# Projection stage of a hybrid attention layer: betas and sums of squares as rows, A ahead of the q convolution, the substitution in buffers of its own

## The chip, the cores and the metric

The kernel runs on one core of one Trainium2 chip. The metric is the device time of one execution in microseconds (us): 16 sequences of 1024 tokens with 256 channels, all in f32 at the interface. A smaller time is better. Engines are called PE (TensorE), DVE (VectorE), ACT (ScalarE), POOL (GpSimd) and SP (SyncE, which only issues DMAs here).

## The reference, cut to what matters

Each sequence passes a delta-rule attention with a router, a slot network, a softmax attention and the slot network again. The change touches the first part of the first one:

```python
q = silu(dw_causal_conv(x @ Wq, conv_q_w))      # 4 taps, k and v alike
beta = sigmoid(x @ Wb)                          # 4 heads of 64 channels
q, k = l2norm(q), l2norm(k); v = v * beta; kb = k * beta
T = -einsum('bhnid,bhnjd->bhnij', kb, k)        # chunks of 32 tokens, strictly lower part
for i in range(1, 32):
    T[..., i, :i] += einsum('bhnj,bhnji->bhni', T[..., i, :], T[..., :, :i])
T = T + eye(32)                                 # inverse of a unit triangular matrix
local_out = dw_causal_conv(v_raw, local_w)      # 7 taps
mid_out = dw_causal_conv(v_raw, mid_w)          # 25 taps
```

## The kernel before

A loop body of some 530 us runs 16 times, once for each sequence. It calls seven stages, each a block in which every engine has its own program, with semaphores between them and a meeting of all engines at the end. `project_and_convolve` (L399 to L729) is the first, followed by `delta_rule`. All intermediate tensors stay in SBUF; `bounce` is a buffer in HBM through which blocks change their layout.

PE multiplies the normed input, channels in the partitions, with Wk, Wv and Wq (L539, units of 512 tokens in four PSUM banks; unit u waits for the evacuation of unit u - 4). Between the q units stand the betas (L515), with the input as the stationary operand and four columns moving. ACT evacuates to `pre` (L603) and makes the first tap (L620), DVE the other three (L678), two halves of 128 channels each. The accumulators of k and q share `k_tm`. ACT takes silu (L609) and squares of k and q (L613). PE sums the squares over a head in small products (L509) and forms the gram matrices of k (`gram`, L528, pairs of banks). DVE turns them into `negd`, minus beta over the sum of squares, and multiplies the grams with it into A (L700). For the reciprocal roots POOL raises both sums to the power -1/2 in one instruction (L444). PE transposes k and v to tokens in the partitions (L501), ACT copies them out (L626).

SP's queue is written out by hand, and each wait in it holds all that stands behind it: 32 copies of v into `rep` (L456), four shifts of eight channel groups, 16 for each channel half; A's four diagonal blocks to `bounce` (L465); the gather of all 32 x 32 blocks into `block_a`, one in each partition (L472), which needs `delta_tm`, where v stood; after the substitution the solution X and its transpose XT to `bounce` (L475, L477) and seven scatters back, into `Xd` and `TT` (L483, L485).

The substitution (L391, L393) goes over 31 columns, two dependent DVE instructions each, in `block_a`, X and the scratch `product`. Beside it PE makes the 25-tap convolution as four units of products of 32 columns on `rep` and `stack` (L576), transposes its result (L588), then the 7-tap convolution in four short units and its transposes. ACT keeps each unit (L655) and each transposed piece (L665); the last go to `local_tm`, where X and XT lie, so they wait for `inverse_out`. DVE ends with the transposed copy of X (L711), four sums over heads for the router (L715, L717) and the scaled v (L721, L722). `keep_warm` (L312) issues products whose result nobody reads.

## Time and profile before

| | us |
|---|---|
| median of 3 runs | 8511.21 (8493.76 to 8513.71) |
| profiled execution, as timed | 8544.68 |
| its span, first to last instruction | 8543.0 |
| PE busy | 7615.2 (89%) |
| DVE busy | 4873.9 (57%) |
| ACT busy | 3364.6 (39%) |
| POOL busy | 1774.2 (21%) |
| mean granted clock of PE | 0.937 of 2.4 GHz |

The shares are means over seven stages with different limits. An f32 product stands in the trace as two instructions, and busy PE includes the warming products. All times in rows are us from the start of the span. An arrow names what ended an engine's idle time. A DMA is shown where SP issues it.

### The profile page before, as it was taken

The numbers are of one execution on the slowest core, as the hardware profiler recorded it, in microseconds if no ns is written. First come the engines' busy times: TensorE is split into PE (matmuls) and PEld (weight loads), VectorE is DVE, ScalarE is ACT, GpSimd is POOL, SyncE is SP. The second block draws the span as 40 slices with busy tenths as digits, with TensorE's granted clock in tenths as the row PEclk, the third lists the DMA queues.
The fourth block names the chain that finished last, engine by engine and source line by source line (L and its number), as shares of the span: only waits on it lengthen the run. The fifth ranks groups of instructions, "written<-read, shape, count | busy, mean of one in ns | idle before, by whom it ended". The sixth has DMA issues, their size and how long they took to land. (4 is left out here: it accounts for less than half of the span.)

```text
span 8543.0 us, 124391 instructions
## 1 busy us (share of the span) xinstructions
PE 7615.2 (89%) x48654; PEld 4524.8 (53%) x48654; DVE 4873.9 (57%) x9442; ACT 3364.6 (39%) x6843; POOL 1774.2 (21%) x2657
## 2 busy tenths in 40 slices
PE   6899988999889889998988998988889988998889
PEld 4546455464654646546464464644646546465464
DVE  5465665556655566554665546655466554655546
ACT  2252532525335253342533425334253342534425
POOL 2112121121211222112221122211222112221212
PEclk9999999999999999999999999999999999999999
DMA  2011111201112021110211102111021110211102
GB/s 71 16 34 27 31 45 22 42 13 31 45 23 43 10 36 40 30 40 8 36 40 31 45 1 36 40 31 45 1 36 40 31 45 1 36 40 31 45 1 41
DMA packets 337643, 268.66 MB, mean 31 GB/s; under 512 B 213378, under 2 KB 276226, under 8 KB 336954
## 3 DMA queue, kind: packets, MB, share of 16 engines
q1 hardware_dynamic: 337004, 260.04, 15.3%
q8 instruction: 414, 6.78, 0.4%
q14 instruction: 225, 1.84, 0.1%
HBM read 48.66 MB, written 42.02 MB: 11 GB/s over the span
## 5 line engine op out<-in xcount | busy, mean ns | idle before, releaser
L1731 ACT ACTIVATE sa_pt<-ps 128x512 f32<-128x512 f32 (+3 forms) x3072 | 1272.0, 492 | 740.3 <-PE ps L1719 734.8
L1656 DVE TENSOR_REDUCE sa_nm<-ps 128x2 f32<-128x1024 f32 (+4 forms) x1280 | 1390.3, 1114 | 285.8 <-PE ps L1637 138.2
L1719 PE MATMUL ps<-sa_qs,sa_ks 99*128 99x512 bf16 (+3 forms) x3072 | 803.4, 336 | 76.1 <-ACT sa_pt L1731 58.3
L1637 PE MATMUL ps<-sa_ks,sa_qs 96*128 96x512 bf16 (+3 forms) x2560 | 642.5, 325 | 47.6 <-DVE sa_nm L1656 33.3
L1738 POOL TENSOR_SCALAR_AFFINE_SELECT sa_pt<-sa_pt 128x512 f32<-128x512 f32 x512 | 325.1, 635 | 1707.7 <-ACT sa_pt L1731 1705.2
L312 PE MATMUL ps<-identb 128*128 128x512 bf16 x2656 | 645.4, 391 | 10.5 <-ACT dr_z L1001 10.5
L1751 PE MATMUL ps<-sa_pt,sa_va 128*17 128x512 f32 (+3 forms) x6144 | 645.8, 492 | 8.2 <-POOL sa_pt L1738 8.2
L1719 PEld LDWEIGHTS ps<-sa_qs,sa_ks 99*128 99x128 bf16 x3072 | 259.3, 98 | 655.4 <-ACT sa_pt L1731 473.7
L576 PE MATMUL ps<-rep,stack 128*32 128x512 f32 x4608 | 501.0, 593 | 0.0
L280 POOL TENSOR_TENSOR rstd<-vare,mhalf 128x2 f32<-128x2 f32 x260 | 181.0, 696 | 1251.2 <-DVE vare L272 1251.2
L797 POOL TENSOR_TENSOR A<-paths 128x256 f32<-128x256 f32 x384 | 272.1, 742 | 802.5 <-DVE paths L967 802.5
L287 ACT ACTIVATE xn<-x,shift,rstd 128x256 f32<-128x256 f32 x520 | 278.2, 592 | 403.7 <-POOL shift L282 403.4
L312 PEld LDWEIGHTS ps<-identb 128*128 128x128 bf16 x2656 | 262.3, 103 | 304.1 <-issue 48.0
L678 DVE SCALAR_TENSOR_TENSOR k_tm<-pre,cw,k_tm 128x1024 f32<-128x1024 f32 x192 | 245.2, 1284 | 226.8 <-ACT k_tm L620 222.2
L1637 PEld LDWEIGHTS ps<-sa_ks,sa_qs 96*128 96x128 bf16 x2560 | 244.4, 99 | 230.2 <-DVE sa_nm L1656 70.1
L1081 DVE COPY ro_partial<-ps 128x512 f32<-128x512 f32 x32 | 22.1, 691 | 558.3 <-PE ps L1113 558.3
L1641 PE MATMUL ps<-causal,identb 128*128 128x128 bf16 x1792 | 339.0, 222 | 0.0
L1219 PE MATMUL ps<-ident,paths 128*128 128x128 f32 x2048 | 269.7, 299 | 67.1 <-DVE paths L1183 67.1
L576 PEld LDWEIGHTS ps<-rep,stack 128*32 128x32 f32 x4608 | 146.5, 110 | 334.9 <-issue 334.9
L319 PE MATMUL ps<-ident,xn 128*128 128x128 f32 x784 | 139.2, 353 | 197.5 <-PEq L1297 77.6
L1175 POOL TENSOR_TENSOR mi_scale<-mi_ms,mhalf 128x16 f32<-128x16 f32 x32 | 92.8, 2899 | 1008.1 <-DVE mi_ms L1188 1008.1
L1219 PEld LDWEIGHTS ps<-ident,paths 128*128 128x128 f32 x2048 | 264.1, 214 | 68.7 <-DVE paths L1183 68.7
(344 smaller groups left out, 14553.2 us busy)
## 6 DMA issues: line engine op xcount, KB each, us to landing
sa_qs<-sa_parts SPq DMA_DIRECT2D x288, 128.0 KB, 4.4
sa_ks<-sa_parts SPq DMA_DIRECT2D x288, 128.0 KB, 5.7
x<-in_x SPq DMA_DIRECT2D x17, 1024.0 KB, 5.6
rep<-paths SPq DMA_DIRECT2D x128, 128.0 KB, 2.3
bounce<-paths SPq DMA_DIRECT2D x32, 512.0 KB, 2.7
out_y<-x SPq DMA_DIRECT2D x32, 512.0 KB, 3.0
rep<-paths SPq DMA_DIRECT2D x128, 127.9 KB, 2.4
rep<-paths SPq DMA_DIRECT2D x128, 127.8 KB, 2.3
```

The source lines that it names most:

```text
L287: return nc.scalar.activation(k.xn[:, t, 0:D], x[:, t, :], ACT.Identity, bias=k.shift[:, t:t + 1], scale=k.rstd[:, t:t + 1])
L312: nc.tensor.matmul(scratch, k.identb[:, 0:P], k.identb[:], start=True, stop=True)
L576: last = nc.tensor.matmul(ps[CG * g:CG * (g + 1), 4 + u % 4, :], k.stack[:, (base + j) * GROUPS + gg, :], rep[:, gg, PAD + n * BANK - SHIF ...
L797: nc.gpsimd.tensor_tensor(with_delta[:, t % 2, 1 + n, :], m.delta_tm[:, t, :], paths[n][:, t, :], ALU.mult).then_inc(s.d_products, 1)
L1219: last = nc.tensor.matmul(ps[:, HALVES * n + a, j * P:(j + 1) * P], paths[i][:, n * TN + j, a * P:(a + 1) * P], k.ident[:], start=(i == 0 ...
L1637: last = nc.tensor.matmul(cols[:, i, :], qs[0:NCOMB * AD, g % NBUF, op.j + i, op.t * P:(op.t + 1) * P], ks[0:NCOMB * AD, g % NBUF, op.j + ...
L1641: last = nc.tensor.matmul(cols[:, i, op.w - P:], k.identb[:, 0:P], k.causal[:], start=False, stop=True, skip_group_check=True)
L1656: nc.vector.tensor_reduce(nm[:, g % 2, op.c, op.t, op.j:op.j + op.heads], cols, AX.X, ALU.max, negate=True).then_inc(s.slot_free, 1)
L1719: last = nc.tensor.matmul(bank[:, off:], ks[0:QROWS, g % NBUF, j, kt * P:(kt + 1) * P], qs[0:QROWS, g % NBUF, j, n * BANK + off:(n + 1) * ...
L1731: nc.scalar.activation(pt[:, gs % 2, j, off:BANK], ring_bank(ring_use(gs, j))[:, off:], ACT.Exp, scale=RATIO).then_inc(s.ring_out, 1)
L1738: nc.gpsimd.affine_select(block, block, [[0, GH], [1, P]], ALU.is_ge, 0.0, base=0, channel_multiplier=-1).then_inc(s.masked, 1)
L1751: last = nc.tensor.matmul(ps[2 * AD * j:2 * AD * j + AD + 1, SUM_BANK, off:BANK], va[:, kt, g * GH + j, :], pt[:, gs % 2, j, off:BANK], st ...
```

## The change

Heads now stand in the partitions and tokens along the row: `wb`, padded to 32 columns, is stationary, the input moves 512 tokens at a time, and the four products (two halves of tokens by two halves of channels) go to four strips of 32 partitions of one bank. The sums of squares do the same with `ones2` of 32 columns, added for k onto the betas' rows. ACT copies these rows to SBUF (`keep_rows`), and a product with the selector `pick` turns them into tokens in the partitions (`pick(i)`).

k's sums are taken, A is made, and only then DVE convolves q, whose accumulator is now `mid_tm`. On ACT silu of k moves among the v pieces. On SP A's blocks leave after the first 16 copies; the gather goes into the scratch part of `TT` (the memory of `pre`, so it waits for q's convolution) and stands ahead of the last eight copies. The first pair of DVE's sums moves ahead of the substitution, q's sums are read after its 16th column, POOL's power becomes one instruction for k and one for q. At the end `Xd` is scattered before `TT`, 7-tap units are ordered by token halves, and their transposes and copies come in two halves. In the core of the diff new lines prevail; lines that went are in the code above.

```diff
...
+    return (*two_squares(TT.rearrange("p t n -> p (t n)")[:, 0:2 * CHUNK * CHUNK]),
+            *two_squares(m.local_tm.rearrange("p t d -> p (t d)")))
...
+    accs = [channel_major(m.k_tm[:]), channel_major(m.v_tm), channel_major(m.mid_tm)]
+    BEHIND = 2 * (3 + L) + 2
+    sq = [channel_major(m.local_tm),
+          pre[:].rearrange("p i a l -> p (i a l)")[:, BEHIND:BEHIND + HALVES * L].rearrange("p (a l) -> p a l", a=HALVES)]
...
+    ROWS, PICKED = (7, 0), (6, 1)
...
+    units = [(0, a, n) for a in range(HALVES) for n in range(NB)] + [(1, a, n) for n in range(NB) for a in range(HALVES)]
...
+            pool.wait_ge(s.rows_ps, 1)
...
+            pool.wait_ge(s.ss, 1)
+            nc.gpsimd.tensor_tensor(m.rn[:, 0, :], m.ss[:, 0, :], k.mhalf[:, 0:T * H], ALU.pow).then_inc(lc.rnorm, 1)
+            pool.wait_ge(s.turned, T)
+            pool.wait_ge(s.rep0, 16 * SHIFTS * (P // CG))
+            pool.wait_ge(s.rep1, 16 * SHIFTS * (P // CG))
+            nc.gpsimd.memset(Xd[:], 0.0).then_inc(lc.zeroed, 1)
+            pool.wait_ge(s.rows_ps, 2)
+            nc.gpsimd.memset(TT[:, scratch:], 0.0).then_inc(lc.zeroed, 1)
             pool.wait_ge(s.ss, 2)
-            nc.gpsimd.tensor_tensor(m.rn[:], m.ss[:], k.mhalf[:].rearrange("p (i n) -> p i n", i=2),
-                                    ALU.pow).then_inc(lc.rnorm, 1)
+            nc.gpsimd.tensor_tensor(m.rn[:, 1, :], m.ss[:, 1, :], k.mhalf[:, 0:T * H], ALU.pow).then_inc(lc.rnorm, 1)
             pool.wait_ge(lc.inverse, 1)
-            nc.gpsimd.memset(Xd[:], 0.0).then_inc(lc.zeroed, 1)
+            nc.gpsimd.memset(TT[:, 0:scratch], 0.0).then_inc(lc.zeroed, 1)
...
+            copies(0, range(SHIFTS))
             sp.wait_ge(s.a, T)
...
-            sp.wait_ge(s.rep0, 16 * SHIFTS * (P // CG))
+            copies(1, range(SHIFTS // 2))
             sp.wait_ge(s.blocks_out, 16 * BLOCKS)
-            block_a = substitution_tensors(m)[0]
-            sp.wait_ge(s.turned, T)
+            sp.wait_ge(s.conv, 3 * HALVES)
             sp.dma_start(block_a, bounce[0].rearrange("b g r c -> (b g) r c")).then_inc(lc.blocks, 16)
+            copies(1, range(SHIFTS // 2, SHIFTS))
...
-            sp.dma_start(bounce[2].rearrange("b g r c -> (b g) r c"), XT).then_inc(lc.inverse_out, 16)
-            sp.wait_ge(lc.inverse_out, 32)
-            sp.wait_ge(lc.zeroed, 2)
+            sp.dma_start(bounce[2].rearrange("b g r c -> (b g) r c"), XT).then_inc(lc.turned_out, 16)
+            sp.wait_ge(lc.inverse_out, 16)
+            sp.wait_ge(lc.zeroed, 1)
+            for b in range(BLOCKS - 1):
+                left = CHUNK * (b % 2)
+                sp.dma_start(by_blocks(Xd, 2 * CHUNK)[rows(b), :, left:left + CHUNK],
+                             bounce[1, b].rearrange("g r c -> r g c")).then_inc(lc.inverse_in, 16)
+            sp.wait_ge(lc.turned_out, 16)
+            sp.wait_ge(lc.zeroed, 3)
...
+            def betas():
+                for n in range(NB):
+                    for a in range(HALVES):
+                        nc.tensor.matmul(ps[rows(2 * n + a), ROWS[0], :], k.wb[:, a, :],
+                                         k.xnT[:, a, n * BANK:(n + 1) * BANK], start=True, stop=False, skip_group_check=True)
+            def sums_of_squares(i):
+                pe.wait_ge(s.squared, HALVES * (i + 1))
+                for n in range(NB):
+                    for a in range(HALVES):
+                        last = nc.tensor.matmul(ps[rows(2 * n + a), ROWS[i], :], k.ones2[:],
+                                                sq[i][:, a, n * BANK:(n + 1) * BANK], start=(i == 1), stop=True,
+                                                skip_group_check=True)
+                last.then_inc(s.rows_ps, 1)
...
+            def pick(i):
+                pe.wait_ge(s.rows, i + 1)
+                for j in range(NT):
+                    last = nc.tensor.matmul(ps[:, PICKED[i], j * PICKS[i]:(j + 1) * PICKS[i]], rows_of[i][:, j * P:(j + 1) * P],
+                                            k.pick[:, 0:PICKS[i]], start=(j == 0), stop=True, skip_group_check=True)
+                last.then_inc(s.picked, 1)
...
-                if i == 0:
-                    pe.wait_ge(s.a, 6)
                 for u in range(T // 2):
-                    if i == 1:
+                    if i == 0:
+                        pe.wait_ge(s.a, (4, 4, 6, 6)[u])
+                        pe.wait_ge(s.pre, 3 * HALVES * NB)
+                    else:
                         pe.wait_ge(s.tm, u + 1)
...
+            betas()
+            for a in range(HALVES):
+                project(2, k.wq, a)
+            sums_of_squares(0)
             pe.wait_ge(s.silu, HALVES)
             gram(0)
+            pick(0)
+            pe.wait_ge(s.pre, 10)
+            gram(1)
             pe.wait_ge(s.pre, 3 * HALVES * NB)
-            gram(1)
-            sums_of_squares(0, 0)
             gram(2)
-            sums_of_squares(0, 1)
-            pe.wait_ge(s.tanh, 1)
-            keep_warm(nc, k, ps[:, AB, :], 6)
+            keep_warm(nc, k, ps[:, ROWS[0], :], 3)
             pe.wait_ge(s.a, 2)
             gram(3)
-            pe.wait_ge(s.ss, 1)
-            for a in range(HALVES):
-                sums_of_squares(1, a)
-            to_token_major(0)
-            to_token_major(1)
-            keep_warm(nc, k, ps[:, AB, :], 4)
+            for i in range(2):
+                to_token_major(i)
+            keep_warm(nc, k, ps[:, ROWS[0], :], 4)
             pe.wait_ge(s.padded, 2)
             pe.wait_ge(s.a, T)
-            pe.wait_ge(s.ss, 2)
...
+                if u == 1:
+                    pe.wait_ge(s.tm, T)
+                    sums_of_squares(1)
+                if u == 2:
+                    pick(1)
+                if u == 4:
+                    pe.wait_ge(lc.evac, 4)
+                    pe.wait_ge(s.ss, 2)
+                    turn_path(0, range(T // 2))
+                if u == 6:
+                    pe.wait_ge(lc.evac, 6)
+                    turn_path(1, range(T // 4))
+            pe.wait_ge(lc.evac, 8)
+            turn_path(1, range(T // 4, T // 2))
             keep_warm(nc, k, ps[:, 4, :], 8)
...
+            def keep_rows(i):
+                act.wait_ge(s.rows_ps, i + 1)
+                nc.scalar.activation(rows_of[i], ps[:, ROWS[i], :], ACT.Copy).then_inc(s.rows, 1)
...
+            for a in range(HALVES):
+                evacuate(0, a)
+                first_tap(0, a)
+            for a in range(HALVES):
+                evacuate(1, a)
+                first_tap(1, a)
+                silu(0, a)
+            silu(1, 0)
+            for a in range(HALVES):
+                square(0, a)
+            silu(1, 1)
+            act.wait_ge(io.stored, 16 * NB)
+            keep_rows(0)
+            evacuate(2, 0)
+            act.wait_ge(s.ss, 1)
+            nc.scalar.activation(by_halves(m.beta[:]), picked(0, 1), ACT.Tanh, scale=0.5).then_inc(s.tanh, 1)
+            first_tap(2, 0)
+            evacuate(2, 1)
+            first_tap(2, 1)
+            to_token_major(0, m.k_tm[:])
+            to_token_major(1, m.v_tm)
+            silu(2, 0)
+            act.wait_ge(s.tm, T)
+            nc.scalar.activation(m.ev[:], m.v_tm, ACT.Square).then_inc(lc.square, 1)
+            silu(2, 1)
+            for a in range(HALVES):
+                square(1, a)
+            keep_unit(0)
+            keep_unit(1)
+            keep_rows(1)
+            keep_unit(2)
+            keep_unit(3)
+            keep_path(0, m.mid_tm, range(T // 2))
+            keep_unit(4)
+            act.wait_ge(lc.summed, 1)
+            act.wait_ge(lc.tm, T // 2)
+            nc.scalar.activation(m.ev[:], m.mid_tm, ACT.Square).then_inc(lc.square, 1)
+            keep_unit(5)
+            keep_unit(6)
+            act.wait_ge(lc.inverse_out, 16)
+            act.wait_ge(lc.turned_out, 16)
+            keep_path(1, m.local_tm, range(T // 4))
+            keep_unit(7)
+            keep_path(1, m.local_tm, range(T // 4, T // 2))
...
-            for i in range(3):
+            for i in range(2):
                 convolve(i)
+            dve.wait_ge(s.picked, 1)
+            nc.vector.tensor_scalar(by_halves(m.ss[:, 0, :]), picked(0, 0), 1e-12, None, ALU.add).then_inc(s.ss, 1)
...
+            settle(nc.vector.reciprocal(m.negd[:], m.ss[:, 0, :]))
...
+            settle(nc.vector.scalar_tensor_tensor(m.negd[:], m.negd[:], -1.0, m.beta[:], ALU.mult, ALU.mult))
...
-            nc.vector.tensor_copy(XT, X.rearrange("p i j -> p j i")).then_inc(lc.inverse, 1)
+            convolve(2)
...
+            def feature_sums(i, path):
                 dve.wait_ge(lc.square, i + 1)
                 nc.vector.tensor_reduce(early[:, :, 3 - i, :], m.ev[:].rearrange("p t (h d) -> p t h d", h=H), AX.X, ALU.add)\
                     .then_inc(lc.summed, 1)
                 nc.vector.tensor_reduce(early[:, :, 1 - i, :], path.rearrange("p t (h d) -> p t h d", h=H), AX.X, ALU.add)
+            feature_sums(0, m.v_tm)
+            dve.wait_ge(s.unit, 2)
+            dve.wait_ge(lc.blocks, 16)
+            settle(substitute(nc, dve, settle, tensors, range(CHUNK // 2)))
+            dve.wait_ge(s.picked, 2)
+            nc.vector.tensor_scalar(by_halves(m.ss[:, 1, :]), picked(1, 0), 1e-12, None, ALU.add).then_inc(s.ss, 1)
+            substitute(nc, dve, settle, tensors, range(CHUNK // 2, CHUNK - 1)).then_inc(lc.inverse, 1)
+            dve.wait_ge(lc.inverse, 1)
+            nc.vector.tensor_copy(XT, X.rearrange("p i j -> p j i")).then_inc(lc.inverse, 1)
...
```

## Rows read from the trace of the kernel before

**Rows 1.** window of the stage: us; busy PE, PEld, DVE, ACT, POOL; clock; DMA; GB/s
```profile
600.00:698.30 98.30, 87.93 (x581) 47.66 (x579) 64.07 (x101) 41.64 (x56) 17.26 (x7) 0.90 0.35 81
```

**Rows 2.** who DVE's substitution waited for, whole span: us, times
```profile
  DMA paths<-bounce: 196.0, 16
```

**Rows 3.** timeline of DVE: start us, us, line, operands, count [idle before <-releaser]
```profile
620.99 7.76 DVE L678 SCALAR_TENSOR_TENSOR paths<-pre,cw,paths 128x1024 f32<-128x1024 f32 x6
...
633.52 3.93 DVE L678 SCALAR_TENSOR_TENSOR k_tm<-pre,cw,k_tm 128x1024 f32<-128x1024 f32 x3 [0.55 <-ACT k_tm L620]
...
639.89 0.19 DVE L692 TENSOR_SCALAR ss<-ps 128x32 f32<-128x32 f32 x1 [2.35 <-PE ps L509]
...
640.94 4.87 DVE L700 TENSOR_TENSOR A<-ps,negd 128x512 f32<-128x512 f32 x8
...
660.95 0.22 DVE L391 TENSOR_TENSOR paths<-paths 128x31 f32<-128x31 f32 x1 [12.55 <-DMA paths<-bounce]
...
673.17 0.43 DVE L391 TENSOR_TENSOR paths<-paths 128x255 f32<-128x255 f32 x1
...
684.39 2.67 DVE L711 COPY paths<-paths 128x1024 f32<-128x1024 f32 x1
...
695.97 2.29 DVE L722 TENSOR_TENSOR x<-paths,e 128x2048 f32<-128x2048 f32 x1
```

**Rows 4.** timeline of SyncE's queue, the same stage
```profile
630.05 21.43 SPq L456 DMA_DIRECT2D rep<-paths  x32
651.53 2.82 SPq L465 DMA_DIRECT2D bounce<-A  x4
656.95 0.34 SPq L472 DMA_DIRECT2D paths<-bounce  x1
...
690.12 0.32 SPq L483 DMA_DIRECT2D paths<-bounce  x1
```

**Rows 5.** timeline of PE, the same stage
```profile
614.60 7.03 PE L539 MATMUL ps<-xnT,wv 128*128 128x512 f32 x16
...
633.88 1.95 PE L509 MATMUL ps<-ones,paths 128*128 128x2 f32 x16
635.75 1.16 PE L528 MATMUL ps<-kT 64*128 64x128 f32 x16
...
648.03 3.50 PE L501 MATMUL ps<-ident,kT 128*128 128x128 f32 x16
...
654.07 24.24 PE L576 MATMUL ps<-rep,stack 128*32 128x512 f32 x224
...
692.71 3.36 PE L588 MATMUL ps<-ident,xn 128*128 128x128 f32 x16 [4.71 <-ACT xn L655]
695.91 1.89 PE L312 MATMUL ps<-identb 128*128 128x512 bf16 x8
```

**Rows 6.** timeline of ScalarE, the same stage
```profile
623.52 1.28 ACT L609 ACT_TABLE_LOAD   x1
...
626.73 1.06 ACT L603 ACTIVATE pre<-ps 128x512 f32<-128x512 f32 x2
627.87 1.15 ACT L620 ACTIVATE k_tm<-pre,cw 128x1024 f32<-128x1024 f32 x1
```

**Rows 7.** busy time of PE in two stretches: us, busy, clock, DMA share, GB/s
```profile
637.00:643.50 6.50, 6.50 (x32) 0.54 0.77 174
651.00:688.00 37.00, 36.28 (x328) 1.00 0.23 54
```

**Rows 8.** timeline in the fourth pass, POOL and DVE
```profile
1702.24 10.54 POOL L444 TENSOR_TENSOR rn<-ss,mhalf 128x64 f32<-128x64 f32 x1 [7.17 <-DVE ss L705]
...
1711.61 0.22 DVE L393 TENSOR_TENSOR paths<-paths 128x31 f32<-128x31 f32 x1
```

**Rows 9.** timeline in the delta rule of the second pass, POOL and DVE
```profile
730.53 2.16 POOL L790 TENSOR_TENSOR dr_squares<-paths 128x256 f32<-128x256 f32 x3
...
731.46 1.52 DVE L936 TENSOR_TENSOR dr_r<-dr_r,x 128x256 f32<-128x256 f32 x1
```

More of the change, by code:

```diff
@@ L145, in _ @@
                     (k.rw2[0:HLAST, HC - 1, :], w["rw2"][(HC - 1) * P:HID]),
-                    (k.rb2, w["rb2"]), (k.gather, w["gather"]),
+                    (k.rb2, w["rb2"]), (k.gather, w["gather"]), (k.pick, w["pick"]),
                     (k.ident, w["ident"]), (b_raw[:, 0:4 * P], w["identb"]),
@@ L420, in out_cm @@
         return k.xn[:, r:r + n // D, 0:D] if n >= D else k.xn[:, r, c:c + n]
-    units = [(c, a, n) for c in range(2) for a in range(HALVES) for n in range(NB)]
+    units = [(0, a, n) for a in range(HALVES) for n in range(NB)] + [(1, a, n) for n in range(NB) for a in range(HALVES)]
     def rows(b):
@@ L459, in _ @@
             sp.wait_ge(s.padded, 2)
-            copies(0)
-            copies(1)
+            copies(0, range(SHIFTS))
             sp.wait_ge(s.a, T)
@@ L490, in _, with project @@
         def _(pe):
+            def project(i, w, a):
+                for n in range(NB):
+                    u = (i * HALVES + a) * NB + n
+                    if u >= 4:
+                        pe.wait_ge(s.pre, u - 3)
+                    for c in range(HALVES):
+                        last = nc.tensor.matmul(ps[:, u % 4, :], w[:, c, a * P:(a + 1) * P],
+                                                k.xnT[:, c, n * BANK:(n + 1) * BANK],
+                                                start=(c == 0), stop=(c == HALVES - 1))
+                    last.then_inc(s.proj, 1)
+            def betas():
[5 more added lines that the diff above has]
+                pe.wait_ge(s.squared, HALVES * (i + 1))
+                for n in range(NB):
+                    for a in range(HALVES):
[9 more added lines that the diff above has]
+                last.then_inc(s.picked, 1)
             def to_token_major(i):
                 pe.wait_ge(s.silu, HALVES * (i + 1))
-                if i == 0:
-                    pe.wait_ge(s.a, 6)
                 for u in range(T // 2):
-                    if i == 1:
+                    if i == 0:
+                        pe.wait_ge(s.a, (4, 4, 6, 6)[u])
+                        pe.wait_ge(s.pre, 3 * HALVES * NB)
+                    else:
                         pe.wait_ge(s.tm, u + 1)
@@ L503, in to_token_major @@
                     last.then_inc(s.turned, 1)
-            def sums_of_squares(i, a):
-                pe.wait_ge(s.squared, HALVES * i + a + 1)
-                for t in range(T):
-                    first = SS[i].start + t * H + 2 * a
-                    last = nc.tensor.matmul(ps[:, SUMS, first:first + 2], sq[i][:, a, t * P:(t + 1) * P], k.ones2[:],
-                                            start=(i == 0 and a == 0 and t == 0), stop=True, skip_group_check=True)
-                last.then_inc(s.sums, 1)
-            def betas(t):
-                for c in range(HALVES):
-                    last = nc.tensor.matmul(ps[:, AB, t * H:(t + 1) * H], k.xnT[:, c, t * P:(t + 1) * P],
-                                            k.wb[:, c, :], start=(t == 0 and c == 0), stop=(c == HALVES - 1),
-                                            skip_group_check=True)
-                if t == T - 1:
-                    last.then_inc(s.beta, 1)
             def gram(u):
@@ L703, in _ @@
                         bc(m.negd[:, 2 * u * H + odd:(2 * u + 2) * H:2], P), ALU.mult).then_inc(s.a, 1)
-            dve.wait_ge(s.sums, 2 * HALVES)
-            nc.vector.tensor_scalar(m.ss[:, 1, :], ps[:, SUMS, SS[1]], 1e-12, None, ALU.add).then_inc(s.ss, 1)
-            dve.wait_ge(s.unit, 2)
-            dve.wait_ge(lc.blocks, 16)
-            substitute(nc, dve, settle, m, range(CHUNK - 1)).then_inc(lc.inverse, 1)
-            dve.wait_ge(lc.inverse, 1)
-            nc.vector.tensor_copy(XT, X.rearrange("p i j -> p j i")).then_inc(lc.inverse, 1)
+            convolve(2)
             early = early_features(m)
-            for i, path in enumerate((m.v_tm, m.mid_tm)):
+            def feature_sums(i, path):
                 dve.wait_ge(lc.square, i + 1)
@@ L2003 @@
     "io": "loaded stored",
-    "pc": "padded proj pre tap conv silu beta tanh turned tm squared sums ss gram a blocks_out unit rep0 rep1",
-    "lc": "blocks square summed conv evac turned tm zeroed rnorm inverse inverse_out inverse_in",
+    "pc": "padded proj pre tap conv silu squared rows_ps rows picked tanh ss gram a turned tm blocks_out unit rep0 rep1",
+    "lc": "blocks square summed conv evac turned tm zeroed rnorm inverse inverse_out turned_out inverse_in",
     "dr": "zeroed products square summed d_products d_square d_summed at_ps at5 at6 y5_ps z "
@@ L2118, in laid_out @@
     i, j = np.arange(P)[:, None], np.arange(P)[None, :]
+    half, wanted, col = (np.arange(4 * H)[None, :] // H) % NB, np.arange(4 * H)[None, :] // (NB * H), np.arange(4 * H)[None, :] % H
+    group, row = i // CG, i % CG
+    of_sum = (wanted == 0) & (row == col % HALVES) & (group == HALVES * half + col // HALVES)
+    of_beta = (wanted == 1) & (row == H + col) & (group // HALVES == half)
     order = (2, 6, 0, 3, 7, 1, 8, 10, 12, 4, 5, 9, 11, 13)
```

171 lines of the change are left out of this document (59 added, 112 removed).

## Prediction

> **What bounds the kernel now.** I read the busy times of one projection stage first [rows 1]. The body runs 16 times and this is its second pass: 98.3 us, in which PE shows 87.9 us and VectorE (DVE) 64.1. PE looks like the bound, but part of its time is warming products and small products that spread over waits for others, so the share doesn't decide. The waits do [rows 2]: DVE sat idle for 196.0 us over 16 passes before the substitution, for a DMA. The reader should see in DVE's timeline [rows 3] one nearly closed chain: v convolution to 628.75, q convolution to 637.45, A from 640.94 to 645.81, then nothing that matters until 660.95, substitution to 684.36, the transposed copy, four sums (8.9 us with the small product behind them), and the scaled v, which ends last at 698.26. In SyncE's queue [rows 4] the hole has a cause: 32 copies of v into rep take 630.05 to 651.48 (0.67 each); A's four block copies stand behind them and leave at 651.53 though A was ready at 645.81; the gather leaves at 656.95, and lands 4.0 later. PE [rows 5] has finished all 224 products of the wide convolution at 678.3, six us ahead of the substitution, and then waits for ScalarE, whose squares wait for DVE. So the stage is set by DVE and SP in turn; PE has little slack. The stage is of one shape in every pass, so a saving counts 16 times.
>
> **The change, from the front.** Times are on the clock of this pass.
> PE's k and v projections end at 614.60 + 7.03 = 621.6 as now [rows 5]. Betas: 8 products on four column strips (the trace shows an f32 product as two). The wide convolution does 224 such in 24.24, 0.108 each, so 0.9. The q projection is now without the small beta products: 16 products at 0.43 = 6.9, to 629.4; as now it ended at 631.9, 2.5 are gained. Sums of squares as rows: 0.9, to 630.3. By then ScalarE has made what they need. The table load (1.3, [rows 6]) and one silu (estimate 1.1, a pass over 1024 as the tap's 1.15) move ahead of the last v pieces, so the last v tap ends at 624.7, which DVE reaches at 624.87: covered by 0.2, no more, and a later one would push the whole chain. Squares are done at about 628.5, silu of v at 629.8.
> The rows then go through ScalarE (0.6) and, behind gram(0), PE (4 picks, 8 products; the sums of squares of now have the nearest form, 16 in 1.95 [rows 5], so 1.0), to 632.3. From the read of the sums to A lie 1.05 now (639.89 to 640.94, [rows 3]), and one operation falls out while beta's comes in: A starts at 633.3. ScalarE meanwhile evacuates q (two pairs of 1.1 about a tap of 1.15 [rows 6], and tanh); its last piece is out at 635.0, and gram(2) waits for it. gram(2), three warming products and gram(3), which also waits for A's bank, follow. At PE's full clock (16 products in 1.1) A ends at 639.2. The rows show the clock at 0.54 in 637 to 643.5 [rows 7], after a stretch of thin products; at the half level gram(2), the warmers and gram(3) take 5.4 instead of 2.8, and A ends at 641.9. I take the middle, **640.5, 5.3 earlier than 645.81**.
> A rule of the Trainium skill bears here (TensorE: Matmul & The Clock Gate, Why this matters for your kernels): don't leave TensorE idle in mid-kernel, or it drops to its lower clock. It speaks against three warmers in place of six. By it A would end at the 641.9 above and everything behind would be 1.4 later, 8.6 a pass and 8373 in all; by the full clock it would be 8330.
>
> q convolution: 2 x 3.93 = 7.8, to 648.3. SP: 16 copies start when silu of v's first half is done, 626.7, and end at 637.4, before A. Block copies 640.5 to 643.3 (2.8, [rows 4]); eight copies to 648.7; gather at 648.7, landed 4.0 later: **652.7**. The last eight copies are issued by 654.4 and landed by 656.7 (2.3 more, as from the last block copy's end at 654.35 to the gather's issue at 656.95). DVE fills the hole: q convolution, then the first two sums, 4.5, to 652.8. So a hole of 12.6 becomes 0, and substitution starts at **652.8 instead of 660.95: 8.1 earlier**. It can't start before 650.7 even with A at 638, nor with the gather as now after 655 if A slips to 643.
> Sixteen columns take 12.2 (660.95 to 673.17), to 665.0, and then DVE wants the second pick. PE: transposes of k after gram(3), 3.5 as now at the half clock, of v half as long, 1.8, warmers 1.0 (eight take 1.9), wide convolution from about 645.5 instead of 654.07, two units of 6.06, row sums 0.9, third unit to 664.6, pick to 665.6. DVE loses 0.7 and 0.2 for the sum; the other 11.2 bring it to **t = 677.2, against 684.36: 7.2 earlier**. PE is now second by under 1 us: here the cover is gone.
>
> **The tail.** Now it takes 13.9 from t. After: DVE has copy 2.67, one pair of sums 4.5, 0.2 and 2.3: t + 9.7. SP: the second solution leaves at t + 2.7 and is out 3.0 later (from the transposed copy's end at 687.06 to the next issue at 690.12, [rows 4]); only then four copies of 0.7 and 2.6 to land: t + 11.1. ScalarE and PE: two copies, the last unit, then at the half clock (3.36 for 16) eight transposes 1.7 and eight warmers 1.9: t + 11.1. The three copies into Xd leave in the gap and cost nothing. POOL's memsets hide behind DVE. I take t + 11.1 with bounds 9.7 (DVE alone) and 12.9 (the warmers at half clock too): **the tail gives 2.8**, bounds 1.0 and 4.2.
>
> Sum: 7.2 + 2.8 = **10.0 us a pass, x 16 = 160 us**. Setup gains one small load and wider weights: nothing against 16 passes. The profiled execution took 8543.0 us of span, 8544.7 as timed; it becomes about 8385. That execution stands 33 above the median of the runs, 8511.2, so the prediction is 8511 - 160 = **8351 us**.
>
> **Rivals.**
> 1. *POOL's power takes DVE's port.* It becomes two instructions of 32 columns, half of 10.54 [rows 8], 5.3 each, one beside the first small products of DVE and one in the middle of the substitution. An addition of DVE with two operands in SBUF, 256 elements wide, took 1.52 when it met a run of POOL's products, and ended 0.3 after the last of them [rows 9]; an operation of that width in the substitution takes 0.43 [rows 3]. If the power acts so, A starts about 5 later but mostly behind the grams, so 2.5 net, and the substitution loses 5.3: 10.0 - 7.8 = 2.2 a pass, 8476. Against it stands [rows 8]: once in this trace the gather came early and the substitution ran for 1.4 us inside the power, its operations 0.22 as ever. That is the last part of a long instruction; its start has not been seen. Chance 0.12. The Trainium skill (SBUF — State Buffer, Who interferes with whom) has this as a rule: a DVE instruction with two SBUF inputs contends with a GpSimd instruction that reads SBUF. Rows 9 agree, rows 8 don't.
> 2. *PE or the queue becomes the bound.* Copies, block copies and the gather share the DMA engines (0.77 busy in [rows 7]); PE starts the wide convolution cold, or rep's second half lands late. Three to six us later at the middle of the substitution: 4 to 7 a pass, 8399 to 8447. For it: PE's slack of 0.7. Chance 0.17.
> 3. *The other side: the clock stays at its half level in the wide convolution.* The three units before the pick, now 18, would take 36: +18 - 10.0 = 8.0 later a pass, 8639. It decides once PE loses more than 10 us there, two units out of three. Against it: the clock was 1.00 in 651 to 688 [rows 7], and these products are dense. Chance 0.03.
> 4. *It does nothing.* The rows' round trip through ScalarE and PE could eat what the order gives: A would have to start 10 later, at 643, which no term above comes near, or several costs meet. Chance 0.04.
> 5. *All goes well*: A at 639.2, PE warm, tail 9.7: 8.5 + 4.2 = 12.7 a pass, 8308; with PE's slack used up little more. Chance 0.10.
> My own case, 8310 to 8395 as its own range: 0.54.
>
> The range takes in 5, the own case and 2, and leaves out 1, 3 and part of 4: **8300 to 8450**. A measurement of this kernel tells 0.3% (26 us) from no change (three runs spread over 20). Faster by more: 0.93 (all but 3 and 4); within 0.3%: 0.04; slower: 0.03.
>
> **What would show it.** DVE's wait for the gather under 2 us instead of 12.6; A's last product near 640; one product of A waiting for gram(2); the power beside substitution operations of unchanged 0.42; PE's wait inside the wide convolution for rep under 1; the stage about 88 long from first projection to the last of DVE instead of 98. Wrong it would be made by a substitution that has a hole of 5 in its middle (rival 1, or the pick late), by granted clock 0.5 after 645, or by a gather that takes well over 4 us beside the copies.

## The result, and the profile after

| | before | changed |
|---|---|---|
| median of 4 runs each, us | 8503.83 (8493.76 to 8513.71) | 8379.37 (8347.73 to 8388.70) |
| profiled execution, as timed | 8544.68 | 8374.86 |
| its span | 8543.0 | 8373.1 |
| mean granted clock of PE | 0.937 | 0.950 |

The ratio is 0.9837, with a 95% interval of 0.9818 to 0.9856: 1.6% faster. The medians differ by 124.5 us, the two profiled spans by 169.9; the profiled execution of before stands 41 above its median, that of the changed kernel 5 below.

The second pass now begins its projections at 590.46, where that of before began at 605.04. DVE's timeline, to be laid beside [rows 3]:

```profile
606.43 7.76 DVE L733 SCALAR_TENSOR_TENSOR paths<-pre,cw,paths 128x1024 f32<-128x1024 f32 x6
618.24 0.19 DVE L745 TENSOR_SCALAR ss<-ps 128x32 f32<-128x32 f32 x1 [4.05 <-PE ps L538]
...
619.07 0.19 DVE L750 SCALAR_TENSOR_TENSOR negd<-negd,beta 128x32 f32<-128x32 f32 x1
619.29 2.48 DVE L754 TENSOR_TENSOR A<-ps,negd 128x512 f32<-128x512 f32 x4
621.93 1.29 DVE L754 TENSOR_TENSOR A<-ps,negd 128x512 f32<-128x512 f32 x2 [0.16 <-PE ps L564]
623.78 1.29 DVE L754 TENSOR_TENSOR A<-ps,negd 128x512 f32<-128x512 f32 x2 [0.56 <-PE ps L564]
624.98 7.76 DVE L733 SCALAR_TENSOR_TENSOR paths<-pre,cw,paths 128x1024 f32<-128x1024 f32 x6
632.66 2.28 DVE L764 TENSOR_REDUCE prob<-x 128x32 f32<-128x2048 f32 x1
634.85 2.27 DVE L766 TENSOR_REDUCE prob<-paths 128x32 f32<-128x2048 f32 x1
639.40 0.21 DVE L388 TENSOR_TENSOR pre<-paths,pre 128x31 f32<-128x31 f32 x1 [2.27 <-DMA pre<-bounce]
...
652.63 0.19 DVE L773 TENSOR_SCALAR ss<-ps 128x32 f32<-128x32 f32 x1 [1.05 <-PE ps L538]
652.74 0.42 DVE L388 TENSOR_TENSOR pre<-paths,pre 128x255 f32<-128x255 f32 x1
...
663.95 2.65 DVE L776 COPY paths<-paths 128x1024 f32<-128x1024 f32 x1
...
671.10 2.29 DVE L782 TENSOR_TENSOR x<-paths,e 128x2048 f32<-128x2048 f32 x1
```

The q convolution and two sums now lie between A and the substitution, in the place of the hole of 12.55. Two small waits are left: 2.27 for the gather, and a new one of 1.05 in the middle, for the second pick (the product with the selector that turns q's sums). Over the span the first is 32.2 us, against the 196.0 of [rows 2]:

```profile
  DMA pre<-bounce: 32.2, 16
```

SP's queue, beside [rows 4]. A's blocks no longer stand behind 32 copies, and the gather no longer behind all of them:

```profile
612.07 10.15 SPq L473 DMA_DIRECT2D rep<-paths  x16
625.09 2.60 SPq L481 DMA_DIRECT2D bounce<-A  x4
627.74 6.32 SPq L473 DMA_DIRECT2D rep<-paths  x8
634.17 0.51 SPq L487 DMA_DIRECT2D pre<-bounce  x1
634.73 4.96 SPq L473 DMA_DIRECT2D rep<-paths  x8
663.94 0.35 SPq L491 DMA_DIRECT2D bounce<-paths  x1
...
669.65 2.64 SPq L503 DMA_DIRECT2D pre<-bounce  x4
```

PE, beside [rows 5]. Betas and both sums of squares take 1.1 each, a pick as much. PE waits 2.53 inside the wide convolution for the last copies of `rep`, and the unit behind that wait takes 7.75, where each unit took 6.06 before. The pick that DVE waits for stands behind both:

```profile
606.99 1.06 PE L523 MATMUL ps<-xnT,wb 128*32 128x512 f32 x8
...
615.05 1.07 PE L530 MATMUL ps<-paths,ones 128*32 128x512 f32 x8
...
617.13 1.07 PE L538 MATMUL ps<-pick,x 128*128 128x16 f32 x8
...
643.78 7.75 PE L609 MATMUL ps<-rep,stack 128*32 128x512 f32 x56 [2.53 <-DMA rep<-paths]
651.46 1.06 PE L538 MATMUL ps<-pick,paths 128*128 128x8 f32 x8
...
672.26 1.89 PE L312 MATMUL ps<-identb 128*128 128x512 bf16 x8
675.12 0.63 PE L893 MATMUL ps<-ident,A 128*128 128x128 f32 x4 [0.97 <-PEq L439]
```

The busy time by windows (us, busy and count of PE, PEld, DVE, ACT, POOL, clock, DMA share, GB/s), to be set against the 0.54 of [rows 7] at the grams:

```profile
612.00:622.00 10.00, 8.57 (x73) 5.25 (x72) 5.62 (x11) 7.86 (x11) 4.59 (x3) 1.00 0.80 181
628.00:634.00 6.00, 6.00 (x58) 1.85 (x60) 5.93 (x5) 4.47 (x5) 0.00 (x0) 1.00 0.87 176
640.00:646.00 6.00, 3.47 (x24) 0.72 (x20) 5.42 (x18) 1.19 (x2) 2.12 (x2) 0.79 0.35 69
643.80:646.80 3.00, 3.00 (x16) 0.77 (x20) 2.76 (x8) 0.00 (x0) 2.92 (x2) 0.50 0.00 0
647.00:652.00 5.00, 5.00 (x49) 1.63 (x41) 4.23 (x11) 0.39 (x1) 0.42 (x1) 1.00 0.00 0
```

The last two rows say why the third unit is long: after its wait PE works without a gap, but for 3 us at half the clock.

And POOL, for the first rival. Both powers run beside DVE's operations of L750 and L388 above, which last 0.19 and 0.42 as ever:

```profile
618.51 5.43 POOL L453 TENSOR_TENSOR rn<-ss,mhalf 128x32 f32<-128x32 f32 x1 [1.14 <-DVE ss L745]
...
652.90 5.53 POOL L462 TENSOR_TENSOR rn<-ss,mhalf 128x32 f32<-128x32 f32 x1 [5.48 <-DVE ss L773]
```

One pass is not the mean, so the next table gives the means over the 16 passes, worked out from the timelines and counted from each pass's first projection product. "Flight" is from the gather's issue to the substitution's first operation; "t" is the substitution's end; "stage" ends where PE begins to load the delta rule's first product.

| kernel | A made | gather issued | flight | subst. starts | 17th column | t | DVE ends | stage |
|---|---|---|---|---|---|---|---|---|
| before | 39.92 | 51.61 | 4.11 | 55.72 | 67.93 | 79.12 | 93.01 | 93.36 |
| changed | 34.34 | 43.47 | 4.94 | 48.41 | 61.76 | 72.95 | 82.43 | 84.35 |
| changed again | 34.60 | 43.81 | 4.98 | 48.79 | 62.20 | 73.39 | 82.88 | 84.75 |
| e1, old tail | 34.43 | 43.65 | 4.89 | 48.54 | 62.04 | 73.23 | 82.74 | 85.75 |
| e2, q before A | 41.91 | 50.88 | 4.98 | 55.86 | 68.35 | 79.55 | 89.04 | 91.62 |
| e3, gather last | 34.30 | 49.23 | 4.23 | 53.46 | 65.79 | 76.98 | 86.43 | 89.62 |
| e4, sum read at 20 | 34.57 | 43.76 | 4.96 | 48.72 | 60.94 | 72.24 | 81.98 | 83.45 |
| e5, last warmers out | 34.18 | 43.40 | 5.04 | 48.44 | 61.75 | 72.94 | 82.42 | 84.00 |
| e6, POOL products | 34.50 | 43.68 | 4.89 | 48.57 | 61.96 | 75.72 | 85.18 | 88.03 |
| e8, gather alone | 34.41 | 43.61 | 3.63 | 47.24 | 64.39 | 75.58 | 85.06 | 87.76 |
| e9, six copies, 20 | 34.49 | 42.49 | 4.75 | 47.24 | 59.46 | 70.78 | 81.60 | 82.15 |
| e10, front warmers out | 33.62 | 42.84 | 4.90 | 47.74 | 61.56 | 72.76 | 82.24 | 84.67 |
| e11, e9 and e10 | 33.73 | 41.72 | 4.78 | 46.50 | 58.71 | 70.00 | 80.85 | 81.22 |
| e12, small products | 39.05 | 47.40 | 7.31 | 54.71 | 67.04 | 78.23 | 87.71 | 90.66 |

The stage went from 93.36 to 84.35: 9.0 a pass, 144 us of the 169.9 by which the spans differ. The rest lies in the other stages, whose code is the same. The medians differ by less than 144; what that leaves open stands below, with the step table.

### The profile page after: what moved, and what is told of

It is laid out like the page before. It is cut to its first block and busy times, and to the rows that moved or that the text cites. A ratio compares the mean times of both kernels' runs of the same rounds, so it can differ in the third digit from the quotient of the medians.

```text
span 8373.1 us, 122632 instructions
## 1 busy us (share of the span) xinstructions
PE 7421.8 (89%) x47710; PEld 4285.2 (51%) x47710; DVE 4866.4 (58%) x9426; ACT 3367.4 (40%) x6875; POOL 1783.2 (21%) x2689
## 5 line engine op out<-in xcount | busy, mean ns | idle before, releaser
L312 PE MATMUL ps<-identb 128*128 128x512 bf16 x2608 | 626.9, 388 | 10.4 <-ACT dr_z L1061 10.4
L609 PE MATMUL ps<-rep,stack 128*32 128x512 f32 x4608 | 529.2, 611 | 41.9 <-DMA rep<-paths 41.9
L312 PEld LDWEIGHTS ps<-identb 128*128 128x128 bf16 x2608 | 253.3, 101 | 297.8 <-issue 42.3
L850 POOL TENSOR_TENSOR dr_squares<-paths 128x256 f32<-128x256 f32 x384 | 283.5, 774 | 0.0
```

Source lines behind the costliest of these rows:

```text
L312: nc.tensor.matmul(scratch, k.identb[:, 0:P], k.identb[:], start=True, stop=True)
L609: last = nc.tensor.matmul(ps[CG * g:CG * (g + 1), 4 + u % 4, :], k.stack[:, (base + j) * GROUPS + gg, :], rep[:, gg, PAD + n * BANK - SHIF ...
L850: nc.gpsimd.tensor_tensor(squares[:, t0 % 2, 1 + n, :], paths[i][:, t0, :], paths[j][:, t0, :], ALU.mult).then_inc(s.products, 1)
```

## The experiments

Each is an edit of the changed kernel. Medians and ratios are against the kernel before on the same chip, whose medians lay between 8510 and 8534 there. The changed kernel itself was run again:

> The changed kernel itself once more, as the standard for the three beside it: 8380 within 10 us, 0.984 of the kernel before.

Measured: 8402.81 us, 0.9872 (0.9857 to 0.9887), stage 84.75, so outside what I expected. The stages agree within 0.4 us, while the ratio lies 0.35 points above the first one. Outside the 16 stages the two spans agree within 1 us, but that of e2 is 29 lower there, that of e5 34 higher and that of before 26 higher, though none of these edits touches the code there. So differences under some 30 us between kernels are read below from the stage, not from the median.

**e1, the old tail.** Scatters interleaved as before, 7-tap units, transposes and copies not in halves.

```diff
-    units = [(0, a, n) for a in range(HALVES) for n in range(NB)] + [(1, a, n) for n in range(NB) for a in range(HALVES)]
+    units = [(c, a, n) for c in range(2) for a in range(HALVES) for n in range(NB)]
...
+                if b < 3:
+                    left = CHUNK * (b % 2)
...
```

> The changed kernel with the end of the stage as before: the scatters into Xd and TT interleaved behind both stores, the 7-tap units in the old order, their transposes and copies all behind the last unit. The stage from the first projection to the first product of the delta rule is 84.35 us as a mean over the passes in the changed kernel and 93.36 before. My theory (the tail by halves gives 2.8 of the 9.0 a pass, since the scatters of Xd leave the path): the stretch from the substitution's end to the next stage goes from 11.4 back to 14.2 and the kernel gets 45 us slower than the changed one, about 8425. Rival (the warmers and the last transposes would hide it): under 10 us slower.

Measured: 8394.91 (8388.16 to 8403.30), 0.9865 (0.9849 to 0.9882). From t to the stage's end 12.52, against 11.40 changed and 14.24 before. So order and halves give 1.1 us a pass. In e1 the last scatter lands 0.46 before the next stage in all 16 passes, and PE ends 4.1 or more ahead of it (8.0 after t, 10.9 in the changed kernel). By the trace, then, the 1.1 come from the scatters' order, and the halves, with the last unit kept behind the wait for the solution, made PE end later. Neither was run alone. The other 1.7 of the tail's 2.8 are there without them: DVE needs 9.5 from t instead of 13.9, since a pair of sums went into the gather's wait. My expectation, that all of the tail's gain hangs on the halves, was too high.

**e2, the q convolution ahead of A.** One line moved.

```diff
+            convolve(2)
             for u in range(T // 2):
...
-            convolve(2)
```

> The changed kernel with DVE's convolution of q ahead of the products into A again; rows, buffers and tail as changed. My theory (the order, not the rows, fills the hole): A ends 7.8 us later, its blocks leave behind it, the gather leaves near 50 us from the stage's start and DVE waits some 8 us for it again; the stage is 7 us longer, the kernel 110 us slower than the changed one, near 8490. Rival (the rows' wide products, done by 16 us earlier, and the gather's new place are what paid): less than 50 us slower.

Measured: 8484.71 (8450.44 to 8511.49), 0.9972 (0.9955 to 0.9988). A comes 7.6 later, the substitution 7.5, the stage 7.3. So without the order on DVE four fifths of the 9.0 are lost.

**e3, the gather behind all copies.**

```diff
-            copies(1, range(SHIFTS // 2))
+            copies(1, range(SHIFTS))
...
-            copies(1, range(SHIFTS // 2, SHIFTS))
```

> The changed kernel with all 16 copies of v's second half ahead of the gather, none behind it. If DVE's chain sets the time, the gather leaves 5 us later (48.5 from the stage's start in place of 43.5), the substitution starts 4 to 5 later, and the wait in its middle of 1.1 us disappears, since rep's second half is there early: 3 to 4 us a pass, 50 to 65 us slower than the changed kernel. If the wide convolution of PE is as much the bound (rival), the earlier copies pay back most of it: under 20 us.

Measured: 8451.28 (8444.65 to 8472.16), 0.9935 (0.9914 to 0.9956). The gather leaves 5.8 later and flies 0.7 shorter, so the substitution starts 5.1 later; 1.0 comes back since the second pick is now early enough (12.3 for 16 columns). The stage is 5.3 longer, more than the 3 to 4 expected, with 1.2 of it behind t.

**e10, no warming products around the last gram.** Seven products of L312 taken out.

```diff
-            keep_warm(nc, k, ps[:, ROWS[0], :], 3)
...
-            keep_warm(nc, k, ps[:, ROWS[0], :], 4)
```

> The changed kernel without the three warming products ahead of the last gram and the four ahead of the wide convolution. In the changed kernel the grams ran at the full clock. If the warmers hold it there, then without them the clock falls to its half level somewhere between the grams and the wide convolution: grams and transposes take up to 5 us more, the second pick comes later and the kernel is 30 to 80 us slower than the changed one. If the wide products of the betas and sums did it (rival), the time is the same within 10 us, and PE is 1.8 us earlier at the wide convolution, which only lengthens its wait for rep.

Measured: 8361.93 (8353.50 to 8369.88), 0.9824 (0.9808 to 0.9841). A is made 0.7 earlier, the clock is 1.00 in each window from 600 to 640, and the stage is as long as before the edit. Why, PE's timeline of this kernel says:

```profile
626.66 12.22 PE L607 MATMUL ps<-rep,stack 128*32 128x512 f32 x112
638.71 1.04 PE L530 MATMUL ps<-pre,ones 128*32 128x512 f32 x8
643.57 7.91 PE L607 MATMUL ps<-rep,stack 128*32 128x512 f32 x56 [3.82 <-DMA rep<-paths]
```

Counted from the pass's start PE is 1.9 earlier at the third unit and waits 1.3 longer for `rep`. The unit behind the wait then takes 7.9, in this pass and as the mean (7.4 in the changed kernel), so of PE's 1.9 the pick keeps 0.1. What makes the pick late is the landing of the last copies and, behind it, a stretch at half the clock.

**e4, the sum read after column 20 instead of 16.**

```diff
-            settle(substitute(nc, dve, settle, tensors, range(CHUNK // 2)))
+            settle(substitute(nc, dve, settle, tensors, range(20)))
```

> The changed kernel, but DVE reads q's sums after column 20 of the substitution instead of after 16. In the changed kernel it waits 1.15 us there for the second pick, which waits for PE's third wide unit, which waits for rep's second half. If that wait is all that PE costs, it disappears: 1.1 us a pass, 17 us in all. Rival (what stands behind the sums on PE, the transposes of the 25-tap path, gets late and gives it back in the tail): no change.

Measured: 8368.44 (8347.73 to 8417.45), 0.9833 (0.9806 to 0.9860). The first 16 columns take 12.2 again instead of 13.4, and the stage is 1.3 shorter than that of the changed kernel beside it: the whole mid wait is gone.

**e9, six copies ahead of the gather and ten behind it, with e4's edit.**

```diff
-            copies(1, range(SHIFTS // 2))
+            copies(1, range(6))
...
-            copies(1, range(SHIFTS // 2, SHIFTS))
+            copies(1, range(6, 16))
```

> As the one before, and only six of the second 16 copies stand ahead of the gather, ten behind it. SP was the last to be ready for the gather (it left at 43.5 from the stage's start, q's convolution ends at 42.2). Expected: gather 1.3 us earlier, the substitution too, 2.3 us a pass with the other, 35 to 40 us below the changed kernel. Rival: the gather is held by the copies' traffic and lands at the same time, then 17 as above.

Measured: 8355.74 (8325.07 to 8363.60), 0.9810 (0.9797 to 0.9824). Against the changed kernel beside it the gather leaves 1.3 earlier, t comes 2.6 earlier, and so does the end. But DVE now waits in the tail:

```profile
665.56 2.29 DVE L764 TENSOR_REDUCE prob<-x 128x32 f32<-128x2048 f32 x1 [1.73 <-ACT x L714]
```

**e8, the gather alone.** The last eight copies wait until it has landed.

```diff
+            sp.wait_ge(lc.blocks, 16)
             copies(1, range(SHIFTS // 2, SHIFTS))
```

> The changed kernel, but the last eight copies of v leave only when the gather has landed. The gather took 4.94 us from issue to the substitution's start as a mean in the changed kernel and 4.11 before, where nothing came behind it. If the copies behind it slow it, it takes 4.1 again and the substitution starts 0.8 earlier, but rep's second half lands 5 us later and the wait in the substitution's middle grows from 1.15 to 5 or more: 50 to 70 us slower than the changed kernel. If the copies ahead of it do (rival), the flight stays at 4.9 and the time is later by the same wait and 10 us more.

Measured: 8457.42 (8422.26 to 8476.29), 0.9913 (0.9885 to 0.9941). The flight is 3.6 in every pass, against 4.6 to 5.9 with the eight copies behind it. Nothing else on the queue ahead of the gather was changed, so the copies behind it are what costs 1.3. The price is paid in the middle of the substitution, where the pick is 5 late (PE waits 4.1 for `rep`, and its third unit takes 8.5):

```profile
642.79 0.22 DVE L388 TENSOR_TENSOR pre<-paths,pre 128x31 f32<-128x31 f32 x1 [0.83 <-DMA pre<-bounce]
...
660.05 0.19 DVE L774 TENSOR_SCALAR ss<-ps 128x32 f32<-128x32 f32 x1 [5.08 <-PE ps L539]
```

**e5, the last eight warming products out.**

```diff
-            keep_warm(nc, k, ps[:, 4, :], 8)
```

> The changed kernel without the eight warming products at the end of the stage. PE ended at 674.15 in the profile and the next stage began at 675.12, when the scatters into TT had landed. If SP's scatters end the stage, the stage's length stays; the delta rule's first products then run at the half clock: 0 to 1 us a pass slower. If PE's end counts (rival), 1 to 2 us a pass faster.

Measured: 8408.96 (8390.82 to 8416.51), 0.9869 (0.9854 to 0.9884). The stage is 84.00 against 84.35 and 84.75, and what comes behind, up to the router's first instruction, takes 89.8 against 88.6 and 89.0. The delta rule's first 3.5 us, from 681.80 in the second pass, run at clock 0.50, in the changed kernel at 1.00. So the warmers cost something in this stage and give it back in the next.

What ends the stage can be read from the landings in the trace. In all 224 passes of the 14 profiles the next stage begins 0.46 after the last scatter has landed, or 0.30 after PE's last product, or 0.31 after DVE's last operation (this one in 14 passes of before), whichever is the latest. In the second pass of the changed kernel it is the scatter, issued at 671.72 and landed at 674.67, and SP's queue waits for it at the stage's end (its waits from 664 to 676: us, times, longest):

```profile
SPq L439 <- DMA pre<-bounce: 2.4, 1, 2.4
```

In the fourth pass it is PE: the transposes take 1.97 instead of 1.09, the warmers 2.67 instead of 1.89, and the clock between 1706 and 1708 is 0.50 (1.00 between 672 and 674):

```profile
1705.14 1.97 PE L573 MATMUL ps<-ident,xn 128*128 128x128 f32 x8 [2.58 <-ACT xn L668]
1706.90 2.67 PE L312 MATMUL ps<-identb 128*128 128x512 bf16 x8
1709.87 0.63 PE L893 MATMUL ps<-ident,A 128*128 128x128 f32 x4 [0.30 <-PEq L439]
```

Over the 16 passes of the changed kernel the scatters end the stage nine times, 10.9 after t, and PE seven times, 12.1 after t. In e5 the scatters do so in all 16.

**e6, products on POOL instead of the power alone.** Behind the second power six products of 128x256, whose result nobody reads, run beside the second half of the substitution.

```diff
+            for n in range(6):
+                pool.wait_ge(lc.rnorm, 2 + n)
+                nc.gpsimd.tensor_tensor(m.side[:, 0, :], k.wq[:, 0, :], k.wq[:, 1, :], ALU.mult).then_inc(lc.rnorm, 1)
```

> The changed kernel with six more instructions on POOL: products of two 128 x 256 constants from SBUF, one behind the other, right after the second power, beside the second half of the substitution. Their result is not used. In the changed kernel the power (5.5 us) ran beside DVE's operations without any effect: 0.42 as ever. If POOL's port is held by instructions that stream from SBUF and not by the power, then DVE's operations beside these products last until one of them ends (0.8 to 1.5 us in place of 0.4) and the substitution gets 2 to 4.5 us longer, 30 to 70 us in all. If DVE and POOL don't disturb each other here (rival), no change.

Measured: 8438.66 (8425.79 to 8470.98), 0.9896 (0.9865 to 0.9928). POOL and DVE in the timeline:

```profile
664.60 5.54 POOL L462 TENSOR_TENSOR rn<-ss,mhalf 128x32 f32<-128x32 f32 x1 [5.53 <-DVE ss L776]
670.21 4.98 POOL L465 TENSOR_TENSOR side<-wq 128x256 f32<-128x256 f32 x6
```

```profile
670.17 0.37 DVE L390 TENSOR_TENSOR paths<-paths,pre 128x207 f32<-128x207 f32 x1
670.58 0.77 DVE L388 TENSOR_TENSOR pre<-paths,pre 128x192 f32<-128x192 f32 x1
671.38 0.78 DVE L390 TENSOR_TENSOR paths<-paths,pre 128x192 f32<-128x192 f32 x1
...
674.59 0.78 DVE L390 TENSOR_TENSOR paths<-paths,pre 128x156 f32<-128x156 f32 x1
675.40 0.30 DVE L388 TENSOR_TENSOR pre<-paths,pre 128x135 f32<-128x135 f32 x1
```

Six operations of DVE go at the pace of POOL's products, 0.77 instead of 0.32 to 0.36; the one before them, inside the power, has its usual 0.37. The second half of the substitution takes 13.76 instead of 11.19.

**e12, betas and k's sums in small products again,** read by DVE and ACT from PSUM as before, the rest as changed.

```diff
+            nc.tensor.matmul(ps[:, 6, t * H:(t + 1) * H], k.xnT[:, c, t * P:(t + 1) * P], k.wb[:, c, H:2 * H], ...)
...
+            last = nc.tensor.matmul(ps[:, 7, t * H + 2 * a:t * H + 2 * a + 2], sq[0][:, a, t * P:(t + 1) * P], k.ones2[:, 0:2], ...)
```

> The changed kernel, but with the betas and k's sums of squares as before: small products between those of q's projection (4 columns moving) and 16 products of 2 columns each for a half, read straight from PSUM; q's sums stay as rows, the order stays as changed. From the rows of before: the betas' products add 2.6 us to q's projection, the sums take 3.9 in place of 1.0, and the copy of the rows and the pick fall out (2.0): A starts 3 to 3.5 us later, the gather too, 50 us slower than the changed kernel. Rival (the round trip through ScalarE and the pick costs what the wide products save): within 15 us of it.

Measured: 8477.19 (8455.04 to 8496.71), 0.9958 (0.9943 to 0.9973), so 74 to 98 us slower than the changed kernel instead of 50. PE in the timeline and by windows:

```profile
626.43 5.58 PE L519 MATMUL ps<-ones,paths 128*128 128x2 f32 x32
631.94 4.29 PE L581 MATMUL ps<-kT 64*128 64x128 f32 x48
```

```profile
626.00:630.00 4.00, 4.00 (x29) 3.93 (x27) 0.00 (x0) 0.00 (x0) 0.00 (x0) 0.75 0.91 210
630.00:634.00 4.00, 4.00 (x28) 3.98 (x30) 1.14 (x4) 1.72 (x4) 1.87 (x3) 0.50 0.58 132
```

32 small products take 5.58 where eight wide ones and a pick take 2.1, PE has no gap in them, and the clock still falls to its half level, where the changed kernel has 1.00. A is 4.7 later and the gather leaves 3.9 later; its flight is 7.3 instead of 4.9, so the substitution starts 6.3 later. The earlier pick gives 1.0 back, and the tail, 1.0 longer, takes it again. Why the flight is so long here is not settled: the queue has the same order, with eight copies in 5.59 ahead of the gather and in 5.58 behind it, where the changed kernel has 6.32 and 4.96.

**e11, e9 and e10 together.**

> The best of the parts together: six copies ahead of the gather, q's sums read after column 20, and none of the seven warming products ahead of the wide convolution. The stage took 84.35 and 84.75 us in the two profiles of the changed kernel, 82.15 with six and 20, 84.67 without warmers (A 0.7 earlier). If the two add up: A and so the gather are no later, the stage is 82 to 81.5, the time 5 to 10 us under that with six and 20, near 8350. Rival (PE's third unit waits for rep's second half, so an earlier PE gains nothing, and the clock falls while it waits): the same or 10 us more.

Measured: 8305.81 (8295.03 to 8355.12), 0.9768 (0.9743 to 0.9794), stage 81.22. This is the fastest version: 2.3% under the kernel before, and its interval lies wholly under that of the changed one. The 0.7 from e10, lost there to the wait for `rep`, is kept here, since the pick is no longer waited for.

## Why the prediction was right, and where it was off

8351 was predicted and 8379 measured, within the likeliest case (8310 to 8395) and its range. Step by step, in us a pass:

| step | predicted | measured, mean |
|---|---|---|
| A made earlier by | 5.3 | 5.6 |
| gather issued, from the pass's start | 43.7 | 43.5 |
| its flight | 4.0 | 4.9 |
| substitution starts earlier by | 8.1 | 7.3 |
| lost at the second pick (before: none), with the sum | 0.9 | 1.1 |
| t earlier by | 7.2 | 6.2 |
| tail shorter by | 2.8 | 2.8 |
| sum | 10.0 | 9.0 |

**The front** came out as worked. A ended inside its bounds, nearer to the full clock: the clock is 1.00 from 605 to 640, where I had taken the middle between the levels. The rule of the Trainium skill that the prediction weighed (TensorE: Matmul & The Clock Gate, Why this matters for your kernels) warns of a TensorE that stands idle between bursts of products. I turned it against fewer warmers, but in this stretch PE was busy for 33.57 of 35 us, and e10 without the seven warmers there keeps 1.00. Where PE did stand idle, 2.5 for `rep`, the trace agrees with the rule: 0.50 from 643.8 to 646.8. That the wide form keeps the clock up at the grams, and not the warmers, e10 and e12 show together: with small products in its place it falls to 0.50.

**The size that was off** is the term "gather issued at 648.7, flight 4.0". The issue was right to 0.2, the flight was 0.9 longer. I took the flight from [rows 4], where nothing stood behind the gather in the queue; in the changed kernel eight copies do. e8 isolates it: 3.6 with the same copies ahead of it and none behind.

**The second pick** came out near its number, 0.9 against 1.1, but not by the path that I had worked out, so that is luck. I had PE at its third unit at 53.5 from the pass's start, behind the landing of `rep` at 51.7, and the sign "PE's wait for rep under 1". Over the passes PE is there at 50.5, waits 2.6 for `rep`, goes on at 53.1, and the unit takes 7.4 instead of 6.06 (e3, with a wait of 1.2, and e2, with 1.7: 6.2; e8, with 4.1: 8.5). With 6.2 the pick would end at 60.3 by my estimate, just ahead of DVE, which asks for it at 60.6; it ended at 61.5. So the step that the prediction lacked is the clock that PE loses while it waits.

**The total.** The stage accounts for 144 us and for 138 in the second profile of the changed kernel; the medians differ by 124.5 and 115.2. These 20 us and more are not explained: there is one profile of the kernel before, 41 above its median, and what the other executions spent in which stage was not recorded. The sign "the stage about 88 long instead of 98" had a wrong base: 98.3 is the width of the window of [rows 1]; from the first projection to the last of DVE before takes 93.0, the changed kernel 82.4.

**The tail's** size was right, and its makeup nearly as worked: DVE 9.7 predicted and 9.5 measured from t, and two ends behind it, both of which I had at 11.1. Where the scatters are last the stage ends at 10.9, where PE is last at 12.1, and which it is changes from pass to pass. The bound of 12.9, with the warmers at the half clock too, was a real case: in e3, e6 and e8 PE ends the stage in all 16 passes, in e2 and e12 in 14, and that is their 0.7 to 1.2 more. In e3's second pass the eight warmers take 3.62:

```profile
683.06 3.62 PE L312 MATMUL ps<-identb 128*128 128x512 bf16 x8
```

What decides in which passes the clock falls there is not shown.

**The rivals.** The first, POOL's power holding DVE, is refuted in place: 16 passes with the power beside the substitution's second half, which takes 11.19 as before. e6 shows that the harm exists, but for products: 2.6 a pass. The Trainium skill (SBUF — State Buffer, Who interferes with whom) has DVE's second port shared with GpSimd as an exclusive lock; the trace agrees for the products (0.77 for 0.36) and not for the power (0.42 either way). The second rival was there in small, 1.1 instead of 3 to 6; e8 shows the same mechanism at 5, and e4 removes it. The third had a beginning: after PE's wait the clock was 0.50 to 646.8. It ended there, back at 1.00 from 647, and cost 1.3 of the 18 that the rival had. The fourth fell with the table of means.

## What to carry to other kernels

Look for an engine's hole and ask which of its own later work doesn't need what it waits for: with q's convolution ahead of A again, 7.3 of the 9.0 us a pass are gone (e2), with the same instructions. Then read the queue behind a transfer as well as what stands ahead of it: the copies behind the gather lengthened its flight by 1.3, and when their landing is what the next engine wants, a faster PE only waits longer and comes back at half the clock (e10), until the reader is moved as well (e11). A small result that is read in the middle of a closed chain is read as late as the chain allows; four columns later was worth 0.9 to 1.3 (e4 against the two profiles of the changed kernel).

## What the runs showed that was not expected

- A power of 128x32 on POOL, 5.4 us, leaves DVE's operations with two inputs in SBUF as they are; a product of 128x256 on POOL, 0.83 us, holds each to about its own length.
- A gather of 32 x 32 blocks took 3.5 to 3.7 in e8, 4.6 to 5.9 with eight copies of 128 KB issued behind it, and 6.2 to 8.4 in e12, unexplained. With nothing behind it the kernel before and e3 still spread from 3.3 to 5.3.
- PE's clock fell to half while PE was busy without a gap, in products of two moving columns (e12), and stayed at full in wide products on 32 stationary columns. It also fell after PE had waited 2.5 for a transfer, and the next 3 us of the same wide products ran at half the clock.
